# A two-layer decoder on one core: identity matmuls on TensorE between stages, later output turns on VectorE, no GpSimd drains in token stages, and router logits computed with held weights

## The reference, cut to what matters

```python
x = ln(x + self_attention(x))            # layer 0: 8 heads forward-causal, 8 backward, linear biases
x = ln(x + cross_attention(x, ctx))      # layer 0: scores clipped at +-10000
s = softmax(xt @ router_w)               # 8 logits for each token; top 2 chosen
h = gelu(xt @ w1) * (xt @ v1); y = h @ w2
x = ln(x + sum_k weight_k * y[expert_k] + bias)
x = ln(x + self_attention(x))            # layer 1: all keys
x = ln(x + cross_attention(x, ctx))      # layer 1: no clip
h = x + latent_causal_attention(rms(x) * g1)
x = ln(x + h + moe(rms(h) * g2))         # logits = t @ gate_w, top 2, silu experts
```

## Time and profile before

| | |
|---|---|
| median of 3 runs | 2065.91 us (2062.48 to 2072.31) |
| the profiled execution's own time | 2067.45 us |
| its span, first to last instruction | 2065.7 us |
| granted TensorE clock, mean over the span | 0.934 |
| PE busy | 1849.5 us |
| DVE busy | 1310.1 us |
| ACT busy | 970.4 us |
| POOL busy | 571.0 us |

### The profile page before, as it was taken

One profiled execution on the slowest core, in us unless ns is written; L12 is line 12 of the kernel. 1 busy time (PEld: TensorE's weight loads), 2 busy tenths in 40 slices (PEclk: granted clock), 3 DMA queues, 4 the chain that ended last, 5 costly groups with the idle time before them and its releaser, 6 DMA issues. The chain is left out here.

```text
span 2065.7 us, 34219 instructions
## 1 busy us (share of the span) xinstructions
PE 1849.5 (90%) x11790; PEld 1057.6 (51%) x11791; DVE 1310.1 (63%) x2305; ACT 970.4 (47%) x1898; POOL 571.0 (28%) x955
## 2 busy tenths in 40 slices
PE   8799998777789999969999999978888999986996
PEld 4344445322689999934222222243343444465995
DVE  4588866777633333367988888455687788754113
ACT  3366663566112222243677777733423666632334
POOL 3211123333234333222011111133453111143551
PEclk9899999789689999989999999997997999987998
DMA  7634405400911111065322230064035343051224
GB/s 183 141 89 66 67 2 126 92 17 2 377 52 36 33 33 36 26 169 127 65 32 32 41 48 7 1 150 83 18 73 123 62 63 60 5 204 39 69 71 143
DMA packets 99097, 158.15 MB, mean 77 GB/s; under 512 B 31447, under 2 KB 79063, under 8 KB 93783
## 3 DMA queue, kind: packets, MB, share of 16 engines
q1 hardware_dynamic: 87122, 131.79, 27.8%
q0 software_dynamic: 7488, 20.46, 3.2%
q10 hardware_dynamic: 4352, 4.20, 0.6%
HBM read 110.67 MB, written 44.72 MB: 75 GB/s over the span
## 5 line engine op out<-in xcount | busy, mean ns | idle before, releaser
L1958 ACT ACTIVATE arena<-psum 128x512 f32<-128x512 f32 (+1 forms) x1120 | 577.0, 590 | 286.8 <-PE psum L1914 202.0
L1671 DVE TENSOR_REDUCE arena<-psum 128x1 f32<-128x1024 f32 (+7 forms) x384 | 428.8, 1156 | 83.8 <-PE psum L1629 49.3
L1914 PE MATMUL psum<-arena 99*128 99x512 bf16 (+7 forms) x1280 | 373.6, 355 | 6.4 <-ACT arena L1958 3.5
L1629 PE MATMUL psum<-arena 96*128 96x512 bf16 (+7 forms) x1280 | 355.4, 360 | 24.4 <-SPq L2668 10.6
L1932 PE MATMUL psum<-arena 128*32 128x512 f32 (+3 forms) x2560 | 280.7, 538 | 0.8 <-ACT arena L1958 0.7
L2391 PEld LDWEIGHTS psum<-arena 128*128 128x128 f32 x2340 | 275.9, 193 | 7.5 <-ACT arena L2438 3.5
L2391 PE MATMUL psum<-arena 128*128 128x128 f32 x2340 | 277.0, 276 | 2.2 <-ACT arena L2438 1.4
L2484 DVE COPY arena<-arena 128x1536 f32 (+1 forms) x117 | 97.2, 831 | 283.6 <-PE psum L2391 281.2
L1657 DVE CUSTOM_DVE_ANT_0 arena<-psum,arena 128x1024 bf16<-128x1024 f32 (+3 forms) x224 | 216.7, 1019 | 47.2 <-PE psum L1629 47.1
L1914 PEld LDWEIGHTS psum<-arena 99*128 99x128 bf16 (+1 forms) x1280 | 119.6, 99 | 236.9 <-ACT arena L1958 137.0
L1629 PEld LDWEIGHTS psum<-arena 96*128 96x128 bf16 (+1 forms) x1280 | 111.3, 100 | 181.7 <-DVE arena L1657 42.2
(11 more groups left out here) (204 smaller groups left out, 2257.9 us busy)
## 6 DMA issues: line engine op xcount, KB each, us to landing
arena<-k_parts SPq DMA_DIRECT2D x144, 128.0 KB
q_halves<-arena SPq DMA_DIRECT2D x80, 192.0 KB, 2.9
arena<-q_halves SPq DMA_DIRECT2D x40, 384.0 KB, 4.9
arena<-in_L_ffn_up SPq DMA_DIRECT2D x8, 1408.0 KB, 17.9
arena<-q_halves SPq DMA_DIRECT2D x40, 256.0 KB, 5.3
k_parts<-arena SPq DMA_DIRECT2D x48, 192.0 KB, 3.2
arena<-in_L_ffn_down SPq DMA_DIRECT2D x9, 1024.0 KB, 14.1
arena<-y_rows SPq DMA_DIRECT2D x32, 256.0 KB, 4.4
```

Source lines behind the costliest of these rows:

```text
L1629: last = nc.tensor.matmul(dst[:, base + lo:base + hi], q[0:rows, qh, h, qb % 4 * P:qb % 4 * P + P], k[0:rows, h, key0 + lo:key0 + hi], sta ...
L1671: nc.vector.tensor_reduce(dst, src, AX.X, ALU.max).then_inc(t("taken"), 1)
L1914: last = nc.tensor.matmul(b[:, at0:at0 + width], kk[0:rows, h, kb * P:kb * P + P], q[0:rows, qh, h, c0:c1], start=True, stop=diag is None)
L1958: nc.scalar.activation(probs[k % at.ahead][:, heads[0]:heads[-1] + 1, c0:c1], bank[st_bank[no % 3]][:, 0:len(heads) * width].rearrange("p ...
```

## The change

1. `keep_running`: after its drain in 14 of the stages, PE computes identity times identity, 9 to 55 times, into a bank that nobody reads then, before it waits for the next stage.
2. An OT is planned 2 us after the mix is thought to be ready, where a DVE operation is to be had before it; `turns_before` makes POOL's mix wait for exactly the turn that frees its rows, where it waited for both turns of the pair of groups.
3. POOL is "undrained" in all token stages.
4. A logits unit holds the router's weights (padded from 8 to 32 columns on the host) and moves 512 tokens: two matmuls, into partitions 0 to 31 and 32 to 63. ACT copies the result out (`act_flat`), PE turns it back by four transposes (`pe_turn`), and DVE adds the two halves.
5. In the cross-attentions DVE's maximum is negated as it is taken, which leaves out a POOL instruction (L1767) of each split in xa0.
6. The store of the context values goes behind the load of job 1's maxima on SP.

The planners' costs change with it (a split 1.9 us, landing 4.0 us in the cross-attentions), so that other orders come out of the search.

```diff
+    def due(self, time):
+        return bool(self.turns) and self.turns[0][0] + 2.0 <= time
+    def behind(self, j):
+        return bool(self.turns) and self.turns[0][1] < j
...
-        moves, queue = [], MixQueue(self.events, 2.5 if self.clip else 1.75)
+        moves, queue = [], MixQueue(self.events, 1.9)
...
         def turn_until(time):
             queue.mix_until(time)
-            while queue.turns and queue.turns[0][0] <= max(free["DVE"], time):
-                mixed, j = queue.turns.pop(0)
-                self.events.append(("OT", j))
-                on_dve(mixed, 0.72)
+            while queue.due(max(free["DVE"], time)):
+                turn_next()
...
                 elif kind == "logits":
-                    for n in range(4):
-                        for c in range(DC):
-                            last = nc.tensor.matmul(ps[:, n * NX:n * NX + NX], xt[:, c, n * P:n * P + P], mat[:, c, :],
-                                                    start=(c == 0), stop=(c == DC - 1))
+                    for c in range(DC):
+                        last = nc.tensor.matmul(ps[32 * c:32 * c + 32, :], mat[:, c, :], xt[:, c, :],
+                                                start=True, stop=True)
...
+            def act_flat(act, u):
+                act.wait_ge(t("work_ps"), u + 1)
+                wait(act, t("turned"), u - 1)
+                nc.scalar.activation(flat_logits[0:64, u % 2, :], work_bank(u)[0:64, :], ACT.Copy).then_inc(t("flat"), 1)
+            def pe_turn(pe, u):
+                pe.wait_ge(t("flat"), u + 1)
+                for n in range(4):
+                    last = nc.tensor.transpose(work_bank(u)[:, 64 * n:64 * n + 64],
+                                               flat_logits[0:64, u % 2, n * P:n * P + P], ident[0:64, 0:64])
+                last.then_inc(t("turned"), 1)
...
-                    dve.wait_ge(t("work_ps"), u + 1)
-                    nc.vector.tensor_copy(o[2][:, half * 4 * NX:half * 4 * NX + 4 * NX], ps[:, 0:4 * NX])\
+                    dve.wait_ge(t("turned"), u + 1)
+                    nc.vector.tensor_reduce(o[2][:, half * 4 * NX:half * 4 * NX + 4 * NX].rearrange("p (t e) -> p t e", t=4),
...
-            if source == "comb":
-                progs["undrained"] = "pool"
+            progs["undrained"] = "pool"
...
-                if at.clip:
-                    nc.gpsimd.tensor_scalar(m[0:32, :], m[0:32, :], CLAMP / QSCALE, None, ALU.min)\
...
-                wait(pool, t("turned"), 2 * (g // 2))
+                wait(pool, t("turned"), self.turns_before(j))
...
-                if early_sp:
-                    early_sp(sp)
                 if not at.moved_early:
                     maxima.load(sp, 0)
                 for g in range(ng):
                     maxima.load(sp, 2 * g + 1)
+                    if g == 0 and early_sp:
+                        early_sp(sp)
...
+        idle_bank = {"t0": 2, "at0": 4, "t1": 2, "xa0": 4, "rt0": 7, "ex0": 6, "t3": 2, "at1": 4, "t4": 2, "xa1": 4,
+                     "t5": 0, "mla": 4, "rt1": 7, "ex1": 6}
+        idle_turns = {"t0": 20, "at0": 11, "t1": 27, "xa0": 11, "rt0": 26, "ex0": 55, "t3": 15, "at1": 11, "t4": 12, "xa1": 11,
+                      "t5": 9, "mla": 11, "rt1": 22, "ex1": 38}
+        def keep_running(pe, name):
+            if name == "t5":
+                pe.wait_ge(sem("att_taken"), len(mla.early) - 1)
+            for _ in range(idle_turns[name]):
+                nc.tensor.matmul(bank[idle_bank[name]][:, 0:P], ident, ident, start=True, stop=True)
...
+                if key == "pe" and name in idle_turns:
+                    keep_running(eng, name)
```

More of the change, by code:

```diff
@@ L292, in on_dve, with turn_next @@
             return free["DVE"]
+        def turn_next():
+            mixed, j = queue.turns.pop(0)
+            self.events.append(("OT", j))
+            on_dve(mixed, 0.72)
         def turn_until(time):
             queue.mix_until(time)
-            while queue.turns and queue.turns[0][0] <= max(free["DVE"], time):
-                mixed, j = queue.turns.pop(0)
-                self.events.append(("OT", j))
-                on_dve(mixed, 0.72)
+            while queue.due(max(free["DVE"], time)):
+                turn_next()
         while n_st < len(st) or n_mx < len(mx) or n_pv < len(self.steps) or moves:
@@ L373, in plan @@
                     queue.mix_until(float("inf"))
+                    while queue.behind(j - 1):
+                        turn_next()
                     self.events.append(("OC", j))
@@ L499, in plan @@
                 taken.append(on_dve(free["PE"] + 0.2, 0.3))
-                landed[j] = queue.split(taken[-1]) + 3.5
+                landed[j] = queue.split(taken[-1]) + 4.0
                 moved = j + 1
@@ L859, in make_plan @@
                         needs.append(("latent", list(lats)[half]))
-                    task("PE", "unit", u, {"klat": 0.9, "vlat": 0.9, "logits": 1.6}.get(kind, 1.75), 0.2, *needs)
+                    task("PE", "unit", u, {"klat": 0.9, "vlat": 0.9, "logits": 0.95}.get(kind, 1.75), 0.2, *needs)
                     if kind == "latent":
@@ L870, in make_plan @@
                         task("SP", "store", u, 0.9, 3.0, ("third", u))
+                    elif kind == "logits":
+                        task("ACT", "flat", u, 0.65, 0.15, ("unit", u), ("turn", u - 2))
+                        task("PE", "turn", u, 0.5, 0.2, ("flat", u))
+                        task("DVE", "evict", u, 0.25, 0.15, ("turn", u))
                     else:
-                        task("DVE", "evict", u, 0.25 if kind == "logits" else 0.8, 0.15, ("unit", u))
+                        task("DVE", "evict", u, 0.8, 0.15, ("unit", u))
                 if following:
@@ L1054, in pool_prog @@
                         following.maxima.pool_split(pool, 0)
+                if any(kind == "more" for kind, n in plan.get("POOL", [])):
+                    pool.wait_ge(t("pool_x"), n_pairs)
             def act_root(act, p):
@@ L1226, in pe_prog @@
                         pe_unit(pe, n)
+                    elif kind == "turn":
+                        pe_turn(pe, n)
                     elif kind == "ckey":
@@ L1753, in dve_move @@
                 if at.clip:
[L1754 to L1755 removed]
+                    nc.vector.tensor_scalar(m_f2[j % 2][0:32, :], self.region(turn)[0:32, 0:P], CLAMP / QSCALE,
+                                            -CLAMP / QSCALE, ALU.min, ALU.max).then_inc(t("taken"), 1)
                 else:
[L1757 removed]
+                    nc.vector.tensor_copy(m_f2[j % 2][0:32, :], self.region(turn)[0:32, 0:P])\
                         .then_inc(t("taken"), 1)
@@ L1799, in dve_take, with turns_before @@
                 nc.vector.reciprocal(orec2[j % 2], self.blocks[:, :, HD]).then_inc(t("rec"), 1)
+            def turns_before(self, j):
+                g, qh = self.at.jobs[j]
+                if g < 2:
+                    return 0
+                last = 2 * (g // 2) - 1
+                return 2 * (g // 2 - 1) + [q for n, q in self.at.jobs if n == last].index(qh) + 1
             def pool_mix(self, pool, j):
```

19 lines of the change are left out of this document (9 added, 10 removed).

## The result

The changed kernel takes 2033.58 us (median of 4 runs, 2031.56 to 2036.32) where the kernel before took 2065.47 us (4 runs, 2062.48 to 2072.31). The ratio over the runs is 0.9837, with a 95% interval from 0.9816 to 0.9858 (the two medians alone give 0.9846), so it is faster by 32 us, clear of the noise. Forecast were 2021 us in a range from 1995 to 2043, a gain of 46.5 us. The profiled execution took 2031.56 us, 2 us under the median, as that of before was 2 us over its own; so the two profiles differ by 35.9 us.

A forecast was written before the change was run, and what follows sets the result against it. It took PE as the bound where dense, PE and DVE in turn in xa0, with boundaries costing a wait plus half-clock work. Terms 15.7 + 11 + 6 + 3.3 + 4.5 + 6.0 = 46.5 us off 2067.45 gave 2021 us, range 1995 to 2043.

The forecast's parts named there:

- The price of the identity matmuls: At stage boundaries: 0.118 us a pass, 0.237 a turn at full clock; clock given back is worth 15.7 us, ends 5 and 22.
- The rival in which they run at half clock: At boundaries: a turn takes 0.47 us and overruns, so the kernel gets slower, 2096 us; chance 0.04.
- xa0, 2 us,: Start of xa0: of 5.3 us at half clock DVE leaves 4.1, POOL still clears semaphores and writes zeros; 2 us taken.
- mla, 4 us: Start of mla: 20.73 us busy at half clock would give 10.4, DVE leaves at most 5.6; 4 us taken.
- at1: Start of at1: 9.26 us busy at clock 0.50, DVE busy for half of that stretch; gain 4.6 us.
- Later turns: Later output turns in the cross-attentions: 11 us in xa0 (ends 4, 16), 6 in xa1 (0, 13); free in self-attentions.
- the mix is ahead of the split and has five DVE operations of 0.7 to 0.8 us to end in: In xa0: the new order lets 11 of DVE's 13.9 us of waits for POOL's mix go.
- No drain on POOL: At t4's end into xa1: waits of 10.0 us for POOL against 6.7 for SP into xa0; gain 3.3 us, or 0.
- The store: In at0 at group 1's load: moving the 1024 KB store of context values saves 4.5 us, ends 1 and 8.
- The sign of a wait under 2 us: In at0: PE's wait for the load of group 1, 6.0 us before, would fall under 2 us.
- Router: Logits and start of t2 with rt0 and t6: 3.5 and 2.5 us, 6.0 in sum, ends 0 and 8, through held clock.
- The rival that the new logits stay at 0.50: In t2 and t6: logits still at half clock, term only 1.7 us, so 2025 us; chance 0.07.

The follow-up runs named there:

- the fifth: Changed kernel without the 16 POOL additions of the next stage's bias row in xa0: 2028.25 us, ratio 0.982.
- eleventh experiment: Changed kernel with groups 1 and 2 planned as landing later, 24 identity matmuls behind t4, xa0's bias additions moved into t2: 2024.4 us, ratio 0.981.
- the nine kernels: The kernels with the changed kernel's order and all its work in xa0; there xa0 took 139.0 to 145.9 us, 142.5 on average.
- The third experiment: Changed kernel with the planners' rules and split costs of before in all five attentions: 2047.23 us, ratio 0.9915.
- second experiment: Changed kernel without the identity matmuls: 2040.42 us, ratio 0.988.
- tenth experiment: Changed kernel with each identity matmul replaced by two transposes of the identity: 2032.25 us, ratio 0.9834.

## Why the prediction was right, and where it was not

The direction and the range held: 31.9 us came in the medians and 35.9 in the profiles, of 46.5. The first cause was read rightly: boundaries cost twice, and filling them gives back clock. Two of the six terms, the store and the drain, brought nothing that can be measured. Step by step:

- **The price of the identity matmuls: right; their worth right in sum, in part by luck.** 24 passes behind t4 took 2.94 us, 0.12 us each. In nine of the 14 places they ran at full clock and ended within 0.5 us of the next opening. Behind t4 they ended 3.0 us ahead of it, behind ex0 and ex1 9.5 and 5.5 after it, and behind rt0 and rt1, where they begin at half clock as foretold, 5.0 and 3.9 after it. The rival in which they run at half clock is out. The term was 15.7, and the part alone gave 14.4 us. But by stages the places that the term named (at1, mla, xa0, t1, t4, t5) gave 9.0 us in that kernel, and xa1, t2 with rt0, and ex1 with t7, which it left out, gave 4.7. Inside it *xa0, 2 us,* gave nothing: 152.1 us with the matmuls alone against 151.5, and 141.9 with all against 141.4 without them. *mla, 4 us,* is refuted (0.3 us longer in after, 1.6 shorter with the matmuls alone): its first 23.7 us still have only 0.71, and DVE is busy for 19.31 of them. *at1* gave 1.9 of 4.6, though its clock was 1.00: 9.26 us of PE at half clock became 8.51 at full clock with more work in them, DVE at 7.49 of 9.60 us. So DVE seems to bound there next; that is read from the windows and wasn't tried. ex1 and t7, put down at 0, gave 2.8; the two kernels with no fill have 187.5 and 187.3 us there, the twelve with fill 183.5 to 186.5.
- **Later turns: the wait read rightly, POOL's work priced at nothing.** 13.9 us of waits fell to 0.8, and 9.6 us came out for xa0 where 11 and 2 were forecast. Of the 3.4 us that are missing, 2 are the term of the identity matmuls above. The step that failed is "the mix is ahead of the split and has five DVE operations of 0.7 to 0.8 us to end in": it counted POOL's work as free for DVE. Mix and bias addition now fall on clips and stretch them by 6.0 us; the fifth and eleventh experiment show this. So the 11 came out too well for its working: 13.1 us of waits less 6.0 us of longer clips are 7, yet xa0 gave 9 on average over the nine kernels. The third experiment has the old order and xa0 still 5.2 us below before, so part of the gain isn't the order's; where it comes from is open, and that the term nearly held is luck. xa1, without clips, gave 7.7 of a forecast 6, and there the order gave all of it. (Its upper end of 13 us was written as 0.15 x 104.9, which is 15.7; 0.15 x 87.47, the busy time, is 13.1.)
- **No drain on POOL: the wait shrank by more than forecast, and its worth is not measurable.** The 3.3 us were the difference of two waits; with the drains back, t4 alone loses 5.6 us and xa1 returns 3.6. The prediction stopped at the stage's opening and did not ask what xa1 then waits for.
- **The store: wrong, 4.5 us forecast, nothing found.** The step "The 1024 KB store takes part of that" took 1 MB at the measured rate off a wait. The store's own issue to landing did shrink from 11.4 to 6.4 us, but the load landed at 91.67 us instead of 91.4, with DMA as full as before although the store was issued only at 87.75. As PE came earlier behind the identity matmuls, the wait grew to 7.6 us: without them it is 6.0 with the store behind (second experiment) as it was with the store ahead. The sign of a wait under 2 us did not come. DMA issues from 76 to 92 us in after:

```profile
vx<-arena SPq DMA_DIRECT2D x1, 1024.0 KB, 6.4
```

- **Router: right in sum, by luck in t6.** t2 with rt0 and t6 gave 2.9 and 3.1 us of 3.5 and 2.5. But with the old logits put back only t2 grew, by about 2 us; t6 kept its gain, which so has another cause that isn't shown. The rival that the new logits stay at 0.50 is refuted: t2 ran at 0.95. The rule of the Trainium skill on transposes, by which the prediction called this rival the likelier way though it gave it 0.07, isn't borne out (tenth experiment). A unit took 1.05 us for the logits, the upper of the two ends given, and 0.46 for its transposes back where 0.95 was forecast, because each is one pass and not two. That DMA would bound t2 and rt0 held, just: in after ex0 opened at 558.09 us, right behind the landing of the last store of token rows at 558.04. It landed 51.8 us behind t2's opening, and 51.1 to 52.8 in all 14 kernels, however long t2 was. But DVE's own work in rt0, which ends 20.5 to 20.7 us behind t2 in every kernel, ended at 558.0 too; in before it alone was the bound, with the last landing 3.7 us ahead of it. What the prediction missed, the 4.28 us of PE's wait for ACT, cost little under this bound.

Of the gap between 46.5 us and the 35.9 of the profile, 4.7 is the store, 4.3 mla, 3.4 xa0 and 2.7 at1; the other stages brought 4.5 more than forecast. What stays open is why the parts overlap by 5 to 8 us in the run times: the stages name xa1 for 2, and the rest is no larger than what one stage differs by between executions.

## What to carry to other kernels

Filling PE's gaps at boundaries pays where dense PE work follows and PE bounds it; count the half-clock time only there, and count the next engine's busy time in the same window first. When work is moved on an engine whose instructions share something with another's, price it on both: here an addition or a mix of POOL that was under way when a clip began cost DVE up to its whole length, and one that came second waited itself. And a stage that opens earlier is only worth what its own first loads allow, so look at the end of the stage behind it.

## What was not expected of the hardware

- A DVE instruction of two inputs in SBUF (0.68 us) lasted up to 1.99 us behind two of POOL's (0.63 us each), the sum of all three; begun first, it kept its length and POOL's took 0.95 us.
- A transpose of the float32 identity took one pass of 0.12 us where a float32 matmul of the same shape took two, and it held the granted clock like one: 133.3 us at half clock with matmuls, 146.5 with the same number of passes of transposes, 217.2 without fill. The other kernels made from after, with matmuls as fill, have 125.2 to 162.3, so 146.5 is within what they differ by.
- An issue of a DMA on ACT, of a store of token rows, lasted 5.33 us while DMA was at 0.98, where the others took 0.37, and held up the two copies queued behind it. ACT in after at the end of t2:

```profile
528.46 0.37 ACTq L969 DMA_DIRECT2D x_rows<-arena  x1
529.87 5.33 ACTq L969 DMA_DIRECT2D x_rows<-arena  x1
535.30 1.08 ACT L1128 ACTIVATE arena<-psum 64x512 f32<-64x512 f32 x2 [4.84 <-issue]
```
